# Last stage of a fused graph and expert kernel: pairs of scatter-adds, and a transposed second product that is turned back

## The reference

```python
affinity = jax.nn.softmax(logits, axis=-1).transpose(0, 2, 1)
gating, index = jax.lax.top_k(affinity, k)               # k = 1250 // 16 * 2 = 156
x_in = jnp.take_along_axis(x[:, None, :, :], index[..., None], axis=2)
h = jax.nn.gelu(jnp.einsum('bekd,edh->bekh', x_in, w1) + b1[None, :, None, :])
x_e = jnp.einsum('bekh,ehd->bekd', h, w2) + b2[None, :, None, :]
weighted = gating[..., None] * x_e
out = out.at[jnp.arange(Bx)[:, None], idx_flat].add(vals_flat)
```

## Time and profile before

| | us |
|---|---|
| median of 3 runs | 2626.36 |
| lowest, highest | 2622.93, 2626.94 |
| the profiled execution | 2644.3 |
| its span, first to last instruction | 2642.6 |
| first transposes of gathered rows in the last stage | 2393.68 |
| last matmul of the stage issued, DVE follows | 2625.99 |

### The profile page before, as it was taken

The page is one execution under the profiler, slowest core; times in us unless marked ns, Lnnn a source line. Parts: engine busy times, 40 slices in busy tenths (PEclk is TensorE's granted clock), DMA queues, the critical chain, the costliest instruction groups (busy, mean ns, idle before and its releaser), DMA issues. The chain is left out here.

```text
span 2642.6 us, 36122 instructions
## 1 busy us (share of the span) xinstructions
PE 2096.5 (79%) x10849; PEld 1293.6 (49%) x10850; DVE 1575.0 (60%) x2490; ACT 951.1 (36%) x1768; POOL 773.6 (29%) x707
## 2 busy tenths in 40 slices
PE   4888888888884563999974397999999999436786
PEld 1444444444442563777731244776346874234453
DVE  1289999999995158333346766776566772262111
ACT  4744444444441221555520214663006660011110
POOL 3176676776762000444453000000000000002333
PEclk7989888888887755999988698999999999658899
DMA  4555555555554320677644313000012001254673
GB/s 132 164 136 133 135 132 135 135 133 136 134 134 93 126 108 2 237 261 272 196 131 124 108 41 102 20 19 17 22 42 62 21 1 66 80 189 125 175 210 58
DMA packets 206222, 300.27 MB, mean 114 GB/s; under 512 B 114695, under 2 KB 126674, under 8 KB 202038
## 3 DMA queue, kind: packets, MB, share of 16 engines
q0 software_dynamic: 98272, 142.08, 19.6%
q1 hardware_dynamic: 107862, 157.06, 18.8%
HBM read 243.72 MB, written 54.96 MB: 113 GB/s over the span
## 5 line engine op out<-in xcount | busy, mean ns | idle before, releaser
L565 POOL DMA_INDIRECT p_s<-node_table,p_srci x320 | 467.3, 1460 | 146.1 <-issue 74.2
L1956 PE MATMUL g_psO<-g_h,g_ring 125*125 125x257 f32 x1600 | 373.0, 388 | 20.3 <-DVE g_ring L2088 11.0
L708 PE MATMUL p_psM<-p_msg,p_to 125*32 125x384 f32 x648 | 290.8, 605 | 82.4 <-DVE p_msg L627 43.9
L1956 PEld LDWEIGHTS g_psO<-g_h,g_ring 125*125 125x125 f32 x1600 | 297.1, 190 | 92.9 <-DVE g_stage L2082 26.5
L585 ACT ACTIVATE p_w<-p_psW 125x512 f32<-125x512 f32 x320 | 187.8, 587 | 369.0 <-PE p_psW L700 369.0
L700 PE MATMUL p_psW<-e_w,p_hid 64*125 64x512 f32 x640 | 272.0, 656 | 20.4 <-DMA p_hid<-hidden 7.7
L627 DVE TENSOR_TENSOR p_msg<-p_w,p_s 125x1536 f32<-125x1536 f32 x160 | 273.4, 1750 | 0.0
L712 PE MATMUL p_psM<-p_msg,p_to 125*32 125x256 f32 x648 | 248.6, 473 | 0.0
L711 PE MATMUL p_psM<-p_msg,p_to 125*32 125x256 f32 x648 | 241.0, 460 | 0.0
L710 PE MATMUL p_psM<-p_msg,p_to 125*32 125x256 f32 x648 | 222.8, 478 | 0.0
L590 ACT ACTIVATE p_of<-e_node_ids,e_rise 125x314 bf16<-125x314 f16 x320 | 176.8, 553 | 8.8 <-PE p_psC L717 5.9
(11 more groups left out here) (342 smaller groups left out, 3869.5 us busy)
## 6 DMA issues: line engine op xcount, KB each, us to landing
p_ring<-in_L_ffn_weights SPq DMA_DIRECT2D x32, 1025.0 KB, 7.4
slot_rows<-p_y POOLq DMA_DIRECT2D x70, 256.0 KB, 4.6
p_w1s<-in_L_ffn_w SPq DMA_DIRECT2D x16, 1024.0 KB, 8.6
p_w2s<-in_L_ffn_w SPq DMA_DIRECT2D x16, 1024.0 KB
hidden<-p_h SPq DMA_DIRECT2D x40, 250.0 KB, 3.4
p_hid<-hidden SPq DMA_DIRECT2D x160, 62.5 KB
g_rb<-receiver_rows SPq DMA_DIRECT2D x16, 610.4 KB
p_x<-x SPq DMA_DIRECT2D x3, 2500.0 KB
```

The lines of the kernel that those rows point to most:

```text
L565: pool.indirect_dma_start(s[:, b, c, :, :].rearrange("p k u -> p (k u)"), None, node_table, bass.IndirectOffsetOnAxis(ap=srci[:, b, c:c + ...
L708: nc.tensor.matmul(psM[i][0:32, 0:3 * MUL], a, rows_[:, 0:3, :], start=begin, stop=end)
L1956: last = nc.tensor.matmul(psO[0:P, j, 0:HW], ring[:, i % RING, j * P:(j + 1) * P], h[:, s, hd, :], start=s == 0, stop=s == T - 1)
```

## The change

The second product is computed transposed. The stationary side is now a block of `w2s` and the 156 nodes move, so `psY` holds output features by nodes, like `psH`. ACT adds the bias, which now lies one value per partition, on the way to a new tile `yt` (4 activations, `outputs` on ACT). PE then turns `yt` back into rows, `rows_back`, 8 transposes into a new PSUM tile `psB`, and DVE scales from there into `y`. The bias tile `b2s` becomes [128, W, 4]. `yb` and its addition are gone.

The two halves of an expert are added to `out` without a wait between them. Only the first half waits, for both adds of the expert before. DVE's writing of `y` waits in the same way once per expert.

`rows_back` of expert e-1 stands in PE's turn e, between `products(e+1)` and `results(e)`.

```diff
@@ sync: loads
-                            sp.wait_ge(yb_ok, 2 * (e - W + 1))
+                            sp.wait_ge(yt_ok, 2 * (e - W + 1))
                         sp.dma_start(w2s[:, u, :, :], w2[bass.ds(e * H, H), :].rearrange("(k p) h -> p k h", p=128))\
                           .then_inc(w2_in[u], 16)
-                        sp.dma_start(b2s[:, u, :], b2[bass.ds(e, 1), :].broadcast_to([CH, D])).then_inc(w2_in[u], 16)
+                        sp.dma_start(b2s[:, u, :], b2[bass.ds(e * 128, 128), :]).then_inc(w2_in[u], 16)
@@ gpsimd
                     for c in range(2):
                         pool.wait_ge(y_ok, 2 * e + c + 1)
-
-                        if e or c:
-                            pool.wait_ge(added, 16 * (2 * e + c))
+                        if e and c == 0:
+                            pool.wait_ge(added, 32 * e)
@@ vector
                         for c in range(2):
-                            v.wait_ge(down, 2 * e + c + 1)
-                            if not new:
-                                v.wait_ge(y_ok, 2 * (e - 1))
-                            nc.vector.tensor_tensor(yb[:, b, c, :], psY[0:CH, c, :], b2s[:, u, :], ALU.add).then_inc(yb_ok, 1)
-                            v.wait_ge(yb_ok, 2 * e + c + 1)
-                            if not new:
-                                v.wait_ge(added, 16 * (2 * (e - 2) + c + 1))
-                            nc.vector.tensor_scalar(y[:, b, c, :], yb[:, b, c, :], gate[:, c, bass.ds(e, 1)], None,
+                            v.wait_ge(back, 2 * e + c + 1)
+                            if not new and c == 0:
+                                v.wait_ge(added, 32 * (e - 1))
+                            nc.vector.tensor_scalar(y[:, b, c, :], psB[0:CH, c, :], gate[:, c, bass.ds(e, 1)], None,
                                                     ALU.mult).then_inc(y_ok, 1)
@@ tensor
                     pe.wait_ge(ht_ok, 4 * e + 4)
+                    for m in range(KD):
+                        if m % 2 == 0 and not first:
+                            pe.wait_ge(yt_ok, 2 * e - 2 + m // 2 + 1)
+                        for k in range(KH):
+                            last = nc.tensor.matmul(psY[:, m // 2, (m % 2) * CAP_E:(m % 2 + 1) * CAP_E],
+                                                    w2s[:, u, k, m * 128:(m + 1) * 128], ht[:, b, k, :],
+                                                    start=k == 0, stop=k == KH - 1)
+                        if m % 2:
+                            last.then_inc(down, 1)
+
+                def rows_back(i, u, first):
+
+                    e, b = W * i + u, u % 2
+                    pe.wait_ge(yt_ok, 2 * e + 2)
                     for c in range(2):
                         if not first:
-                            pe.wait_ge(yb_ok, 2 * e - 2 + c + 1)
-                        for k in range(KH):
-                            last = nc.tensor.matmul(psY[0:CH, c, :], ht[:, b, k, c * CH:(c + 1) * CH], w2s[:, u, k, :],
-                                                    start=k == 0, stop=k == KH - 1)
-                        last.then_inc(down, 1)
+                            pe.wait_ge(y_ok, 2 * e - 2 + c + 1)
+                        for m in range(KD):
+                            last = nc.tensor.transpose(psB[0:CH, c, m * 128:(m + 1) * 128],
+                                                       yt[:, b, m, c * CH:(c + 1) * CH], ident[:])
+                        last.then_inc(back, 1)
...
                             products(*ahead(i, u, 1), False)
+                        if not (first and u == 0):
+                            rows_back(*ahead(i - 1, u, W - 1), first and u == 1)
                         results(i, u, first and u == 0)
                 rounds(pe, body)
+                rows_back(TURNS - 1, W - 1, False)
@@ scalar
+                def outputs(i, u, first):
+                    e, b = W * i + u, u % 2
+                    for k in range(2):
+                        act.wait_ge(down, 2 * e + k + 1)
+                        if not first and k == 0:
+                            act.wait_ge(back, 2 * (e - 1))
+                        for m in (2 * k, 2 * k + 1):
+                            last = nc.scalar.activation(yt[:, b, m, :], psY[:, k, (m % 2) * CAP_E:(m % 2 + 1) * CAP_E],
+                                                        ACT.Identity, bias=b2s[:, u, m:m + 1])
+                        last.then_inc(yt_ok, 1)
+
...
                             hidden(*ahead(i, u, 1), first and u == 0)
+                        outputs(i, u, first and u < 2)
```

More of the change, by code:

```diff
@@ L2211, in chosen_experts @@
         b1s = sb("b1s", [128, W, KH])
-        b2s = sb("b2s", [CH, W, D])
+        b2s = sb("b2s", [128, W, D // 128])
         xg = sb("xg", [CH, W, 2, D])
@@ L2215, in chosen_experts @@
         ht = sb("ht", [128, 2, KH, CAP_E])
-        yb = sb("yb", [CH, 2, 2, D])
+        yt = sb("yt", [128, 2, KD, CAP_E])
         y = sb("y", [CH, 2, 2, D])
@@ L2220, in chosen_experts @@
         psY = pb("psY", [128, 2, 512])
+        psB = pb("psB", [128, 2, 512])
         norm = Norm(nc, ctx, "p8_norm", T, eps[:])
@@ L2248, in chosen_experts @@
         down = sem("down")
-        y_free = sem("y_free")
-        yb_ok = sem("yb_ok")
+        yt_ok = sem("yt_ok")
+        back = sem("back")
         y_ok = sem("y_ok")
@@ L2612 @@
     a["L1_ffn_b1"] = by_partition(a["L1_ffn_b1"])
+    a["L1_ffn_b2"] = by_partition(a["L1_ffn_b2"])
     for name in ("L1_gnn_b1", "L1_gnn_b2"):
```

## The result

The changed kernel takes 2705.5 us (median of 4 runs, 2702.9 to 2711.0), before 2624.6 (2622.1 to 2626.9): 1.031 times as long, 95% interval 1.029 to 1.033, some 81 us more. The forecast was 2681, with a range of 2633 to 2708.

What follows compares the result with a forecast made beforehand. POOL, waiting for adds to land, bound the stage at 15.1 us per expert; the change closes a ring of 20.8. Start 2418.0 plus twelve rings 243.3 plus end 35.7 gives 2697.0, carried to the median as 2681; range 2633 to 2708.

Steps and rivals of the forecast that it cites:

- What bounds: Last stage before the change: POOL is waited out, its adds idle 112.6 us for the add before to land.
- The ring: Last stage: turning back, scaling, two adds, two gathers, turning, first product, next turning back; 20.8 us a turn against 15.1.
- what is moved decides: Adds now hang on turning back in PE's next turn, leaving only a 4.28 us second product before the gathered rows' turning.
- The first half of back 0: PE issues the first half of expert 0's turning back at 2418.0 us, where twelve turns of the wait cycle start.
- second gather's flight: From the second gather's issue to its rows' arrival beside weight loads: 7.5 us, between bounds of 3.3 and 8.4.
- first product: PE's first product after the wait for gathered rows: 5.35 us, with 4.28 at full clock as the other end.
- the loaded ring: Main case, last-stage wait cycle with weights loading beside the gathers: time 2668 to 2694 us, chance 0.62.
- clock or pair worse than 2694: Worst case: slow TensorE clock or paired adds delaying gathers bring the time above 2694 us; chance 0.07.
- the gathers escape the weights: Rival: gathers undisturbed by weight loads, 16.6 us a turn, time 2637; wholly or partly (2632 to 2668), chance 0.18.
- the ring does not close: Rival: gathered rows are ready when the second product ends, so 10.0 us per expert, time 2558; faster case, chance 0.08.
- The clock: Rival: TensorE stays at 1.2 GHz through the first product, 8.56 us, 24.0 a turn, time 2719; shares chance 0.07.
- pairs of adds hold up the gathers: Rival: two adds ahead in POOL's queue delay gathers by zero to 1 us a turn, up to 12; shares chance 0.07.

Runs made afterwards that it cites:

- its second profile: Kernel before with only one scalar operation added in the edge stage: ratio to before 0.9995, last stage 242.6 us, 14.5 us per expert.
- the best kernel: Changed kernel with POOL issuing the gathers of expert e+4 ahead of the adds of e: ratio to before 0.9762, last stage 182.8 us.

## Why the prediction was right, and where its size was off

**What bounds.** Right. POOL's waits for landings went from 112.6 to 3.5 us, as the prediction said they would.

**The ring.** Right, and shown by two opposite edits. With the gathers ahead of the adds it opens (10.2 us per expert), with the turning back one product earlier it shortens (12.3). The step "what is moved decides" carried the sign. The first half of back 0 was forecast 24.3 us after the stage's start and came at 24.4; the end from back 12 on was forecast at 35.7 us and measured 35.8 (2667.4 to 2703.2). All of the miss within the stage lies in the twelve rings: 263.5 us measured, 243.3 forecast. Of the profile's signs the ring's were as forecast in kind and a little off in size: PE waited 9.4 to 11.2 us (8 to 10), first adds stood 21.3 to 23.8 us apart (20 to 21), the weights led the second gather by 0.62 to 0.85 us (0.3 to 0.7), and the clock fell to 0.75.

**Their terms.** For the first ten rings, by the prediction's own sum:

| term | forecast | measured |
|---|---|---|
| first half of back to first add | 1.27 | 1.37 |
| first add to second gather | 4.92 | 4.95 |
| second gather's flight | 7.5 | 8.6 (7.98 to 9.78) |
| turning | 1.30 | 1.09 |
| first product | 5.35 | 6.16 (5.38 to 6.98) |
| first half of back | 0.45 | 0.45 |
| ring | 20.8 | 22.6 |

Over all twelve rings the 20 us come from the flight (+13), the first product (+9), the turning (-3) and the first add (+1). The forecast's turning runs to the end of its row, which overlaps the product: from start to start the rows of before give 1.09 and 5.39 us where I added 1.30 and 5.35.

The flight is the first term that was mis-sized. By phase alone I had 8.1, and took 7.5 because no add followed the gathers, a reason that the runs don't bear out. The bound of 8.4 was exceeded too: the nearest rows were two, 7.9 and 8.4, and the ten of after reach 9.8. That the weights are its cause is shown by the two runs without them beside it, and by the last ring of the changed kernel itself, in the chain that ended last:

```profile
2656.99 3.32 DMA p_xg<-rows,p_chosen
...
2660.36 1.01 PE p_psT L2445 x8
2661.36 5.70 PE p_psH L2458 x32
```

3.3 us, forecast 3.3. The first product is the second term. I took 5.35 from one row after one long wait, and kept as a rival that the clock might not come back within the product. The truth lies between 5.35 and the rival's 8.56: 5.38 to 6.98, mean 6.16. The run that kept PE busy shows that this is the clock: 4.28 us again in seven of the first ten rings. The eleventh ring was forecast at 18.7 with a gather of 5.4; it measured 20.7 with 7.4, so one weight tile of the two makes up 4 of the 5 us by which both delay it.

**The carrying over to the median.** The stage's difference, 74.9, is 20 us above the forecast 54.4; the measured difference is 81. The rest, 6 us, may lie in my base, since the profiled last stage of before was 6.3 us longer than in its second profile; that is not shown.

**The range and the chances.** 2705.5 lies 2.5 us under the range's upper end and above the 2694 up to which I had put the loaded ring with a chance of 0.62. It fell where I had written "clock or pair worse than 2694", with 0.07. That the range held is in part luck: one of the four runs, 2711.0, lies above its end of 2708. The mechanism is the loaded ring all the same; what took it above 2694 is the flight first, then the clock, and the 6 us outside the stage, and not the pair.

**The rivals.** That the gathers escape the weights: refuted, with weights sent 0.6 to 0.85 us ahead of the second gather all ten were late. It is what happens if the weights wait (17.1 against 16.6 forecast). That the ring does not close: refuted, and its price confirmed, 10.16 us per expert where I had 10.0. The clock: half right, as said. That pairs of adds hold up the gathers: refuted by the gathers of 3.2 to 3.6 us behind pairs. The price of 2.4 us per transfer of 160 KB that comes of the fit in the Trainium skill (DMA: Bandwidth & Descriptors, Anatomy of one DMA) was met by no gather here: 3.0 us, at the start of the stage in the changed kernel (2378.75 to 2381.75), was the least. That a DMA engine goes round its queues packet by packet, as the Trainium skill says (DMA: Bandwidth & Descriptors, Queues, rings and completion order), would let weights delay a gather, as they did: 8.0 to 9.8 us beside them, 3.2 to 3.6 alone. No run here looks at the packets, so how the delay comes about is not shown.

**DVE** scaling from PSUM took 0.74 us a half where I had 0.69. ACT's four activations were hidden, as forecast.

## What to carry to other kernels

A transfer that is issued behind another in one queue inherits what that one waits for; before a step is moved later, walk on from it through the queue of everything behind it, and count how much work is left between the last of these and its reader. Here a reordering of two lines on POOL turned 3.1% slower into 2.4% faster than before, with the same instructions. And a small transfer started just behind large ones can take nearly as long as they do: here the gather took 8.6 us on average, and the two weight tiles beside it landed 6.6 and 8.8 us after their issue (medians over the stage). Where both hang on one event, let the large one wait.

## What the runs showed of the hardware

- Two gathers behind two accumulating DMAs in one queue land about as fast as behind one: the second is there 3.2 to 3.6 us after its issue (3.2 to 3.4 behind one), and the adds go out 1.83 us apart.
- A gather of 160 KB beside 1 or 2 MB of weights issued 0.6 to 0.85 us ahead takes 7.4 to 9.8 us, more than double; issued 3.9 to 4.7 us behind the start of 2 MB it takes 6.5 to 7.6; 2 to 5 us ahead of them it takes 3.2 to 3.6.
- After waits of 9.4 to 11.2 us the granted clock was back within the first product each time, but not at the same point: the same 32 passes took 5.4 to 7.0 us. After waits of 4.5 to 5.2 us (weights late) they took 5.6 to 6.1, where 4.28 is full clock. A wait half as long spared 0.3 us of 6.16 on average.
- In the loaded part of the best kernel (2424.5 to 2526 us) PE and the DMA engines were both near their end, 0.99 and 0.97 busy, at 265 GB/s.
